# RWKV time mixing and a mixture of experts on one core: two k*v products of a pair of lines become one VectorE instruction

## What is computed

```
def step(S, ins):
    r_t, k_t, v_t, w_t = ins
    kv = jnp.einsum('bhi,bhj->bhij', k_t, v_t)
    y_t = jnp.einsum('bhi,bhij->bhj', r_t, S + u[None, :, :, None] * kv)
    return (w_t[..., None] * S + kv, y_t)
...
x = _layernorm(x + attention(x))
x = _layernorm(x + experts(x))      # 32 experts, top 2
```

## Time and profile before

| what | value |
|---|---|
| median of 3 runs | 2528.02 us (2510.86 to 2529.39) |
| profiled execution, its own time | 2527.71 us |
| its span | 2526.0 us |
| mean granted TensorE clock | 0.891 |
| time mixing, about | 57 to 1455 us of the span |
| VectorE busy over the span | 1948.0 us (77%) |
| TensorE busy over the span | 1981.6 us (78%) |

### The profile page before, as it was taken

The page is one execution under the profiler, slowest core; times in us unless marked ns, Lnnn a source line. Parts: engine busy times, 40 slices in busy tenths (PEclk is TensorE's granted clock), DMA queues, the critical chain, the costliest instruction groups (busy, mean ns, idle before and its releaser), DMA issues. The chain is left out here.

```text
span 2526.0 us, 34986 instructions
## 1 busy us (share of the span) xinstructions
PE 1981.6 (78%) x11174; PEld 1428.1 (57%) x11174; DVE 1948.0 (77%) x3236; ACT 980.7 (39%) x1663; POOL 1282.2 (51%) x762
## 2 busy tenths in 40 slices
PE   5737767867686777677777538999999999999990
PEld 2213333433333333333333228999999999999990
DVE  3949999999999999999999925665666665666645
ACT  2113323322342333333233225545555445555445
POOL 3625656566565556665666432444444444434440
PEclk9968988888898888889888658999999999999995
DMA  3951112111110111121112014544554545544438
GB/s 86 231 119 49 28 42 59 26 36 57 52 31 32 56 25 47 39 55 25 39 35 63 9 36 131 121 117 116 134 125 112 122 114 119 141 115 119 116 61 270
DMA packets 172520, 208.98 MB, mean 83 GB/s; under 512 B 12476, under 2 KB 152160, under 8 KB 172448
## 3 DMA queue, kind: packets, MB, share of 16 engines
q1 hardware_dynamic: 133200, 164.29, 23.5%
q0 software_dynamic: 28672, 34.78, 8.0%
q10 hardware_dynamic: 10576, 9.13, 1.1%
HBM read 118.65 MB, written 75.53 MB: 77 GB/s over the span
## 5 line engine op out<-in xcount | busy, mean ns | idle before, releaser
L1040 POOL TENSOR_TENSOR prod<-S,rT 128x2048 f32<-128x2048 f32 x128 | 536.3, 4191 | 315.1 <-DVE S L820 314.9
L820 DVE TENSOR_TENSOR_SCAN S<-wT,S,vb 128x512 f32<-128x512 f32 x512 | 624.7, 1261 | 0.0
L1238 PE MATMUL up<-x_parts,w_parts 128*128 128x308 f32 x3072 | 464.6, 308 | 1.5 <-DVE x_parts L1349 1.5
L1254 PE MATMUL down<-w_parts,h_parts 128*128 128x256 f32 (+1 forms) x3840 | 464.4, 282 | 0.0
L1254 PEld LDWEIGHTS down<-w_parts,h_parts 128*128 128x128 f32 (+1 forms) x3840 | 458.9, 184 | 2.6
L1238 PEld LDWEIGHTS up<-x_parts,w_parts 128*128 128x128 f32 x3072 | 439.8, 189 | 2.1 <-issue 1.8
L563 PE MATMUL vb<-v_stack,pick_v 128*128 128x512 f32 x512 | 218.7, 513 | 255.9 <-DVE S L820 218.4
L1311 POOL TENSOR_TENSOR ye<-ye,weight 128x256 f32<-128x256 f32 (+1 forms) x160 | 205.8, 1286 | 376.8 <-DVE ye L1401 376.8
L1392 DVE TENSOR_TENSOR h_parts<-h_full,h_parts 128x616 fp32r<-128x616 f32 x256 | 212.5, 830 | 200.8 <-ACT h_parts L1289 200.5
L1289 ACT ACTIVATE h_full<-up,b_now 128x616 f32<-128x616 f32 x256 | 198.7, 776 | 427.9 <-PE up L1238 427.0
L1319 POOL DMA_INDIRECT sums<-ye,sum_at x160 | 280.7, 1754 | 151.1 <-POOL ye L1311 139.1
(11 more groups left out here) (169 smaller groups left out, 2510.6 us busy)
## 6 DMA issues: line engine op xcount, KB each, us to landing
w_raw<-in_L_ffn_w_dram SPq DMA_DIRECT2D x64, 1024.0 KB, 8.8
expert_in_rows<-y_tok SPq DMA_DIRECT2D x10, 1957.5 KB, 27.9
xe<-expert_in_rows SPq DMA_DIRECT2D x32, 522.0 KB
v_stack<-v_parts SPq DMA_DIRECT2D x64, 256.0 KB, 4.5
x_tok<-in_L_attn_x_dram SPq DMA_DIRECT2D x16, 512.0 KB, 4.2
x_res<-in_L_attn_x_dram SPq DMA_DIRECT2D x16, 512.0 KB, 3.5
sums<-x_row SPq DMA_DIRECT2D x16, 512.0 KB, 2.9
rows<-sums SPq DMA_DIRECT2D x16, 512.0 KB, 5.3
```

The source lines that it names most:

```text
L820: dve.tensor_tensor_scan(line[:, 1:TC + 1], wT[:, par, half, :], vb[:, p % 2, g, :], line[:, 0:1], ALU.mult, ALU.add).then_inc(scanned, 1)
L1040: pool.tensor_tensor(prod[:, q % 2], S[:, q % RING, :, 0:TC], rT[:, par, half, None, :].to_broadcast([P, QUAD, TC]), ALU.mult).then_inc(pr ...
L1238: last = pe.matmul(up[:, f % 2, half, 0:HC], w1_parts[:, par, wp, k, f * P:(f + 1) * P], x_parts[:, par, xp, k, half * HC:(half + 1) * HC] ...
L1254: last = pe.matmul(down[0:m, (par * TILES + t) % 2, 0:C], h_parts[:, hp, f, t * P:t * P + m], w2_parts[:, par, wp, f, :], start=(f, n) == ...
```

## The change

The two products of a pair become one instruction on both PSUM banks (128 x 1024), with k broadcast over the two banks. It waits for both fills of `vb`. `kv_done` now counts once for a pair, and only the first of the two scans waits for it.

```diff
-                    for g in range(2):
-                        dve.wait_ge(vb_full, stage_value(i, NU, 2 * p + g + 1))
-                        dve.tensor_tensor(vb[:, p % 2, g, :], vb[:, p % 2, g, :], kT[:, par, half, :], ALU.mult
-                                          ).then_inc(kv_done, 1)
+                    dve.wait_ge(vb_full, stage_value(i, NU, 2 * p + 2))
+                    dve.tensor_tensor(vb[:, p % 2], vb[:, p % 2], kT[:, par, half, None, :].to_broadcast([P, 2, TC]),
+                                      ALU.mult).then_inc(kv_done, 1)
                     if p % 2 == 0:
                         dve.wait_ge(start_set, stage_value(i, NQ, q + 1))
                     for g in range(2):
                         line = S[:, q % RING, 2 * (p % 2) + g, :]
-                        dve.wait_ge(kv_done, stage_value(i, NU, 2 * p + g + 1))
+                        if g == 0:
+                            dve.wait_ge(kv_done, stage_value(i, NPAIR, p + 1))
                         dve.tensor_tensor_scan(line[:, 1:TC + 1], wT[:, par, half, :], vb[:, p % 2, g, :],
                                                line[:, 0:1], ALU.mult, ALU.add).then_inc(scanned, 1)
```

## The result

The changed kernel takes 2558.73 us in the median of 4 runs (2552.13 to 2566.51), the kernel before, run beside it, 2522.04 us (2510.86 to 2529.39). The ratio is 1.0151, 95% interval 1.0095 to 1.0206: 38 us slower by the ratio (37 by the medians) where I had forecast 16. The profiled execution took 2552.13 us, 24.4 above the profiled one of before. The direction was right. The size was not: the added time is more than twice the forecast, and the median lies 0.7 us beyond the upper end of the range. Of all executions behind the numbers of this document one, of `product_early` with 3826.39 us, ran in a slow state and is left out.

What follows compares the result with a forecast made beforehand. VectorE's queue in the time mixing was taken as the bound; 224 x 0.054 = 12.1, 32 x 0.170 = 5.4, start 0.3, less 1.7 gave +16 us on 2527.7: 2543.8 us. Range 2520 to 2558 us.

Steps and rivals of the forecast that it cites:

- What bounds the kernel: Time mixing, 60 to 1455 us: VectorE is busy 94%, so a delay in its queue reaches the end in full.
- One product in place of two: VectorE's products: a pair's two cost 1.197 us now, the merged one lasts 1217 ns, and broadcasting k costs nothing.
- The new wait: First scan behind the merged product: overlap of 0.085 us lost, gap of 34 ns added; 0.054 us more a pair.
- Rival A: At the first scan: the wait costs nothing and the saved start is kept; 16.6 us less, 2511 us; chance 0.10.
- The section of the Trainium skill that the prediction set against its sum: VectorE's starts: none before the pipe empties, semaphore or not, so saving 256 starts would make the change faster.
- Even pairs in the unrolled chunks: First scans of 32 even pairs in four unrolled chunks: a sequencer step waits for the product, 0.170 us more each.
- Rival B: Line 819: the sequencer's step comes at every even pair, 128 in all; 27.3 us more, 2555 us; chance 0.13.
- Both banks at once: Product's wait for both `vb` fills: 5 us of cover, so only the wait near the start grows, by 0.3 us.
- What swallows some of it: At L687 and a chunk's first L693, held up by GpSimd's product: at most 1.7 us given back.
- Rival C: At L687, L682, L708 and chunk ends: existing hold-ups swallow the delay; 2530 us, give or take 4; chance 0.12.
- The sum: Whole kernel: 12.1 + 5.4 + 0.3 less 1.7 gives +16 us, 2543.8 us, 0.6% more.

Runs made afterwards that it cites:

- `product_early`: The changed kernel with the first normalisation's inversion one pair later, plus the next pair's merged product right behind the scans, ahead of all work between pairs: 2548.01 us, 1.0123.
- the pair of kernels without long forms: The kernel before and the changed kernel, each with the first normalisation's inversion one pair later: 2516.05 us (0.9976) and 2531.18 us (1.0034).

## Why the prediction was wrong in size

- **What bounds the kernel**: right. The stage is VectorE's queue, and the added time lies in it whole.
- **One product in place of two**: right. 1217 ns forecast and measured; the broadcast costs nothing that shows.
- **The new wait**: right, 34 ns forecast, and behind a write to PSUM it is the same: 11.3 us less the 32 steps leave 0.035 us for each of 224 pairs. Rival A (2511 us), by which the wait costs nothing, doesn't hold here; the product with a wait behind it starts its scan 1.25 us later and not 1.13, and two products with a late wait lose 30 us by that wait alone. The section of the Trainium skill that the prediction set against its sum ("VectorE: DVE Perf Modes", "The DRAIN you can't avoid") adds that a next instruction which its rule on start partitions doesn't hold back starts earlier, which the prediction left out. What differs from these runs is its other half, that a semaphore costs nothing extra: here one on the instruction right in front costs about 0.12 us, the overlap of 0.088 and the gap of 0.035.
- **Even pairs in the unrolled chunks**: right in number and place (32 steps at line 819, 4 chunks of 8), too high in price: 0.131 us more than before for each and not 0.170. The other 224 pairs pay 0.062 and not 0.054, since the two products had cost 1.191 us in the mean and not 1.197; the two errors nearly cancel (18.1 us for 17.5). Rival B's 128 steps didn't come.
- **Both banks at once**: right for this order. The wait that the prediction places near the start, at the first fill of chunk 1 (159.07 us in the trace of before), went from 31.6 to 31.9 us and there is no other. That it rose by the 0.3 forecast says little, since in the profiles of one order it varies by more than that (31.3 and 31.6 before, 31.9 and 40.6 after). With the product between the scans the cover is gone and the waits come, 52 us of them.
- **What swallows some of it**: too low, 1.7 us. In the pair of kernels without long forms the product path adds 18.0 us, the scans 2.3 and the loop's end 2.8, 23 in all, and 15 arrive between the medians (13 between the profiled executions). So about 8 us are given back: 3.3 at L687 and L710, the others in the waits for the fill in chunk 1, at L682 and at L693. The mechanism of rival C, a delay that goes into waits that are there anyway, was at work for a third of the added time. That 15 us arrive where the sum had 16 is therefore partly luck: 5 us that it hadn't and 6 more swallowed than it had.
- **The sum**: this is where it failed. It took the rest of the stage as fixed, the four waits of 7.0 us in all at L708 among it, as if each cost 1.8 us and would come as often. Each is the tip of 4.14 us, because L710 behind it then meets GpSimd's product, and their number isn't fixed: 4 in the two profiles of before, 6 and 8 in the two of the changed kernel. Two more are 8 of the 24 us between the profiled executions. Eight against four would be 17 of the 36 in the second session, if the kernel before, which has no profile there, had its four. Rival C looked at the same places (L687, L682, L708) and asked only whether they would swallow time, not whether they would make some.
- Smaller: the wait at the loop's end (L667) rose from 11.8 to 14.8 us in five times, 3 us that I hadn't forecast. A pair's two scans take 2.37 us to the next instruction, 0.009 more than before, 2.3 us.
- The range was built on the bounds of the product path, and rival B was its upper end. The spread of the three runs before, 18.5 us, I put down to measurement. It is about four long forms of 4.14 us, and 2511.1 us, the profiled time without its four, is where the fastest run lies (2510.86). The runs without a profile don't show their count, so that reading is an inference; for it speaks that the kernel without long forms spreads by 6.7 us in 12 runs and the kernel before by 19.2 beside it.

**What stays open**: why the changed kernel has more long forms. L477 runs at half clock where the stretch of low clock falls on it; that a change of the stage's pace shifts this is my reading, and no run tests it. TensorE idles for about the same 1.6 us in front of L477 in both forms, so the row in front doesn't decide it. Nor is a low clock there a mark of the merged product: with the later normalisation, L477's mean is 822 ns with two products and 714 with the merged one. That the surplus comes with the long forms was shown by taking them away in both kernels; that they must be more in the changed kernel wasn't, and how many the median run has isn't known.

## What to carry to other kernels

Merging two instructions saves a start only if what follows doesn't need the result at once: in a queue in which, as here, each instruction starts 0.085 us before the end of the last, two small ones with a consumer one step behind beat a large one with the consumer right behind it. Put independent work between producer and consumer, and check what cover that takes from the others: the same product one place further cost 27 us of late fills. And when a stage is bound by one engine, look at each wait that occurs in some rounds of a loop only, follow it to the next instruction of the same engine, and price it as both together; its number may differ from run to run, and a change can go with more of them.

## What the runs showed of the hardware that was not expected

- A wait of the sequencer's own for the instruction in front costs 1.33 - 1.22 = 0.11 us from its end to the next start; one carried by the instruction 0.035.
- Small VectorE instructions on SBUF tiles can be held by a GpSimd instruction for nearly its whole length: 128x4 elements are recorded for 3.29 us beside a GpSimd product of 4.17 us and end with it, and for 0.16 us without one.
- A half clock on four matmuls, 1.74 us more on an engine that isn't the bound, became 4.14 us on the engine that is, through ScalarE's order and GpSimd's product. TensorE's mean clock over the whole run hardly shows it (0.891 and 0.888 for four and six such chunks).
